# Repeating the products of twelve pairs of maximum blocks behind the last expert tile

## What is computed

```python
# convolution stage, per image
x = group_norm(hidden, pre) + pos_emb
gate = sigmoid(conv(silu(conv(silu(conv(x)))))); enhanced = x * gate
sh = group_norm(x, norm)                               # 1024 tokens x 128 channels
standard = attention(sh @ wq, sh @ wk, sh @ wv)        # 8 heads of 16
multi = two attentions of 64: queries from enhanced, keys and values from sh
x = group_norm(out_w(ff_w2(silu(ff_w1([standard, multi])))), post) + hidden
# token attention
t = x as tokens; t = t + attention(layer_norm(t), 8 heads of 16)
# experts
t = t + sum over the 2 chosen of 8 experts of w2(gelu(w1(layer_norm(t))))
```

## Time and profile before

| | |
|---|---|
| median of 3 runs | 3732.41 us |
| lowest and highest | 3728.28 and 3738.99 us |
| profiled execution | 3718.79 us |
| its span (first to last instruction) | 3717.0 us |
| mean granted TensorE clock over the span | 0.901 |
| busy: TensorE, VectorE, ScalarE, GpSimd | 82%, 61%, 47%, 17% |

### The profile page before, as it was taken

One profiled execution on the slowest core, in us unless ns is written; L12 is line 12 of the kernel. 1 busy time (PEld: TensorE's weight loads), 2 busy tenths in 40 slices (PEclk: granted clock), 3 DMA queues, 4 the chain that ended last, 5 costly groups with the idle time before them and its releaser, 6 DMA issues. The chain is left out here.

```text
span 3717.0 us, 43766 instructions
## 1 busy us (share of the span) xinstructions
PE 3063.4 (82%) x15438; PEld 1283.9 (35%) x15438; DVE 2274.4 (61%) x4359; ACT 1743.5 (47%) x2599; POOL 634.7 (17%) x558
## 2 busy tenths in 40 slices
PE   4789787988889898897879888897979978898855
PEld 1225322362223522253223622244322622235225
DVE  4753867457672777538674676737774486746750
ACT  1444354445554455443544455543644445444523
POOL 3010321004010220102210130102201032101322
PEclk9899799998998899997989989997999979898977
DMA  4014320063102620143300621025301532017125
GB/s 94 1 41 147 67 49 18 24 178 60 25 18 69 158 58 2 41 141 67 54 18 24 185 53 25 18 92 135 58 5 38 161 69 34 19 35 192 43 44 163
DMA packets 171289, 252.92 MB, mean 68 GB/s; under 512 B 25899, under 2 KB 79991, under 8 KB 170871
## 3 DMA queue, kind: packets, MB, share of 16 engines
q1 hardware_dynamic: 161791, 230.58, 25.0%
q0 software_dynamic: 9216, 18.89, 2.0%
HBM read 192.55 MB, written 56.83 MB: 67 GB/s over the span
## 5 line engine op out<-in xcount | busy, mean ns | idle before, releaser
L1268 DVE TENSOR_REDUCE blockmax<-ps 128x1 f32<-128x512 f32 x1912 | 1256.0, 685 | 565.4 <-PE ps L689 486.4
L1101 ACT ACTIVATE prob<-ps 128x1024 f32<-128x1024 f32 x1024 | 996.9, 1020 | 619.6 <-PE ps L861 522.2
L689 PE MATMUL ps<-ks,qs 96*128 96x512 bf16 x1656 | 677.6, 421 | 318.9 <-DVE blockmax L1268 205.9
L861 PE MATMUL ps<-qs,ks 99*128 99x512 bf16 x2048 | 653.4, 404 | 10.6 <-DMA qs<-maxrow_dram 7.6
L689 PEld LDWEIGHTS ps<-ks,qs 96*128 96x128 bf16 x1656 | 162.4, 102 | 1029.9 <-DVE blockmax L1268 777.7
L578 POOL TENSOR_TENSOR rs<-vn,vec 128x1 f32<-128x1 f32 (+1 forms) x43 | 42.8, 996 | 1707.9 <-DVE vn L1223 1196.9
L1145 ACT ACTIVATE prob<-ps,b1t 128x128 f32<-128x128 f32 x828 | 235.8, 368 | 164.2 <-PE ps L953 163.9
L861 PEld LDWEIGHTS ps<-qs,ks 99*128 99x128 bf16 x2048 | 206.2, 103 | 281.5 <-issue 88.7
L875 PE MATMUL ps<-prob,va_b 128*32 128x512 f32 x2048 | 291.9, 644 | 0.0
L875 PE MATMUL ps<-prob,va_a 128*32 128x512 f32 x2048 | 286.6, 633 | 0.0
L914 PE MATMUL ps<-qm,km 65*128 65x512 f32 x512 | 270.5, 654 | 3.6 <-ACT prob L1101 3.6
(11 more groups left out here) (227 smaller groups left out, 3315.5 us busy)
## 6 DMA issues: line engine op xcount, KB each, us to landing
shared<-in_w SPq DMA_DIRECT2D x108, 256.0 KB
prob<-in_w SPq DMA_DIRECT2D x108, 256.0 KB, 3.5
parts_dram<-parts SPq DMA_DIRECT2D x34, 768.0 KB, 4.4
ks<-parts_dram SPq DMA_DIRECT2D x204, 128.0 KB, 5.0
qs<-parts_dram SPq DMA_DIRECT2D x204, 128.0 KB, 7.4
qm<-in_w SPq DMA_DIRECT2D x90, 256.0 KB, 3.6
xe<-in_w SPq DMA_DIRECT2D x54, 256.0 KB
oatt<-in_w SPq DMA_DIRECT2D x54, 256.0 KB, 3.3
```

The costliest lines, as they stand in the source:

```text
L689: pe.matmul(ps[:, MX + n % 2, :], lhs, rhs, start=True, stop=True).then_inc(blocks_ready[f], 1)
L861: mm = pe.matmul(ps[:, SC + h, :], ks[:, slot_of(a, g), h, t * P:(t + 1) * P], qs[:, slot_of(a, g), h, cols(q)], start=True, stop=True)
L1101: act.activation(prob[:, n % 3, 2 * pr:2 * pr + 2, :], ps[:, SC + 2 * pr:SC + 2 * pr + 2, :], ACT.Exp, scale=HD ** -0.5).then_inc(exp_done ...
L1268: dve.tensor_reduce(blockmax[:, unit_of(j), cell_of(j), k:k + 1], ps[:, MX + n % 2, :], AX.X, ALU.max).then_inc(blocks_used[f], 1)
```

## The change

Pairs 0 to 15 stay as they are. For each of the pairs 16 to 27 the two products are issued three times, with the same operands and into the same banks. Every product starts its sum anew (`start=True`), so the last round leaves the same numbers. Only the two products of the last round signal `blocks_ready`.

```diff
+                def product(i):
+                    rows = slice(32 * (h + i), 32 * (h + i + 1))
+                    return pe.matmul(early_banks(d)[:, i, :], parts[rows, 1, 0, tile * P:(tile + 1) * P],
+                                     k_even[rows, cols(k)], start=True, stop=True)
+
+                if d >= UNDER_EXPERTS:
+
+                    for r in range(2):
+                        for i in range(2):
+                            product(i)
                 for i in range(2):
-                    rows = slice(32 * (h + i), 32 * (h + i + 1))
-                    pe.matmul(early_banks(d)[:, i, :], parts[rows, 1, 0, tile * P:(tile + 1) * P],
-                              k_even[rows, cols(k)], start=True, stop=True).then_inc(blocks_ready["b"], 1)
+                    product(i).then_inc(blocks_ready["b"], 1)
```

## The result

The median is **3786.25 us** (3778.89 to 3793.19, 4 runs) against 3730.35 us for the kernel before (3724.88 to 3738.99, 4 runs on the same chip). The ratio is 1.0147, 95% interval 1.0115 to 1.0180: slower, and 36 us above the forecast range. The profiled execution took 3778.89 us, with a span of 3777.1 us, 60.1 us more than before, and a mean granted clock of 0.896.

The account below looks back on a forecast made before the run. VectorE's reductions, 1.13 us apart, were taken to bound pairs 16 to 27 and hide the added products. Pair 16's 0.35 us in four images made 1.4 us, taken as 1: median plus 1, 3733 us, range 3718 to 3750.

Parts of the forecast that it names:

- 2.13 - 1.43 - 0.14 = 0.56 us: Pairs 19 on: TensorE's lead less a changed pair's duration and its signal; ready 0.56 us before VectorE wants it.
- The 0.14 us of a signal: From finished product to VectorE's reduction: estimated at 0.05 to 0.14 us from products at 378.77; 0.14 taken.
- the prediction had 0.35: Pair 16, not covered by reductions: ready 0.35 us late, so the last reduction ends 0.35 us later.
- the cover at 1.7 us: Images 1, 2, 6 and 7: GpSimd's own work hides the 0.35 us delay, with a lead of 1.7 us or more.
- the power's lead: Opening of the token attention: VectorE's variance was ready 1.76 us before GpSimd took it in image 1.
- the stall: TensorE's wait in step 2, 5.0 to 6.7 us; predicted to end 0.35 us later in images 3, 4, 5, 8.
- The rounds overlap: Pairs 16 to 27: rounds start 0.40 us apart at 1.2 GHz, so a changed pair lasts 1.43 us.
- The clock: Rival: busier TensorE brings the clock back for the token attention's opening; 3.2 us faster, to 3729; chance 0.09.
- The mix of long and short images: Width-64 attentions: images 1 and 2 went the long way at a lower clock, 7 us more per image.
- clock rival: Width-64 attentions: slow images turn fast (-14 us, 0.11), or more go the long way (+14 us from two, 0.16).
- Rounds that don't overlap: Rival: a pair's six products run one after another, 2.4 us a pair; 108 us slower, 3841; chance 0.02.
- distances other than 430 and 437 us: Sign of a wrong forecast: time from pair 27 to the next image's pair 27 leaving 430 and 437 us.

Follow-up runs that it names:

- the narrow rounds: The change with its two extra rounds 64 columns wide instead of 512, same number of instructions; 3800.60 us, 1.0160 against the kernel before.
- the single signal: The change, with only the last product of each pair signalling, by two at once; 3804.09 us, 1.0138 against the kernel before.
- ScalarE's copies: The kernel before, without extra products, plus 36 one-column copies on idle ScalarE once pair 20 is reduced; 3773.31 us, 1.0064.

## Why the prediction was wrong

**The step that failed.** "I take 0.14. So from pair 19 on each pair is ready 2.13 - 1.43 - 0.14 = 0.56 us before VectorE wants it: 48 products an image at nothing, hidden by the reductions." The 0.14 us of a signal came from a moment at which nothing else of this kind was going on the earlier trace rows. Beside the gather the signal of pair 26 in image 1 came 11.4 us behind its products. The cost is 10.3 us an image ahead of the reductions where the prediction had 0.35. That the gather is needed for it is shown (moved, the idle time falls from 89.9 to 8.9 us, and the same 48 products cost 2.2 us). That it does not go by columns or by signals is shown by the narrow rounds and the single signal; more instructions cost more (28, 69 and 84 us of idle time for 6, 12 and 24 extra products in pairs 22 to 27), but only late in the gather. SyncE's transfers are not needed for it. That it is not in TensorE alone is shown by ScalarE's copies, which are held up themselves and make a signal of TensorE's late behind the pairs. That the copies' slots and the pairs' late signals are one mechanism is argued: both come up only beside the gather.

**The size of what GpSimd hides.** I put the cover at 1.7 us in four images, from the power's lead, and wrote that the power would come as before, 17 us behind the last reduction. It waited for the variance instead (8.09 us in image 1), 13.9 us behind it. The earlier end of the stall gave back 23.5 us over eight images, 3 us in each, but against 82.8.

**What held.** L712 x832. The rounds overlap: 18 products in 2.74 us in image 2, at 1.2 GHz, where six rounds on one row group make 5 x 0.40 + 0.63 = 2.63. Pair 16 waits 0.30 us against the predicted 0.35, in six images; in images 1 and 4 the clock was still up when its products ran (18 products in 1.47 us) and it waits nothing. Image 2:

```profile
828.85 2.74 PE L712 MATMUL ps<-k_even,parts 32*128 32x512 bf16 x18 [1.21 <-DVE blockmax L1287]
...
830.44 2.36 DVE L1287 TENSOR_REDUCE blockmax<-ps 128x2 f32<-128x1024 f32 x2 [0.30 <-PE ps L712]
```

So the prediction's claim that the clock is at 0.50 there in all eight images holds for the kernel before alone. For pairs 16 to 21 by themselves "at nothing" was right: 1.0015, an interval that includes 1. With the gather out of the way the whole forecast fits: 2.2 us between two medians whose intervals overlap, where I had 1.

**The rivals.** The clock: 0.50 while the late pairs run, and 0.54 over the first 10.1 us of the opening where it had been 0.50, so it did not come back for the opening. The mix of long and short images stayed two to five, so neither clock rival came up. Rounds that don't overlap would have shown as long products; they are not. The text itself said that distances other than 430 and 437 us would mean a cost that I miss. That is what they were.

**Open.** What it is that each instruction sends out. Every run here was also recorded by the profiler, so it may be the records themselves, and no run here can tell whether an unrecorded execution would lose the 56 us. The missing events of signals speak for it, since they show the recording in trouble in just this stretch, but they don't show that it holds an engine up. The Trainium skill, page "NOTIFIC — the notification-queue block", section "7.1 Overflow: three behaviours, one of which stalls the engine", says that the internal pipeline of the block that writes such records pushes back on its producers rather than lose one. That would fit engines that stand still while every record of their instructions arrives; the events of signals were lost all the same, and no run here shows which block lost them. Open too is why it is the issuing rather than the landing of the indirect transfers that the late pairs follow (2.9 to 3.3 us behind its end), which was read from the traces and not tried apart. And why pair 24 is the first late one even where pairs 16 to 21 have no extra rounds, and why 96 instructions were free where 60 were not.

## To carry to other kernels

A latency read from a quiet moment, such as the 0.14 us of a signal here, did not hold beside a burst of GpSimd's indirect transfers; look at what every other engine does in the stretch before costing short instructions at nothing. Where an engine is idle, its operands are ready by the records, and the profile gives "remote" or "issue" as releaser, look for gaps in even steps and move the suspected burst away: that one experiment told more than five that varied the suspect. Count the trace's events too: where some are missing, the recording may be part of what is measured. None of these kernels beats the one before; moving the gather behind the pairs clears the signals but costs 2.8%.

## Unexpected behaviour of the hardware

- Beside 16 indirect transfers of GpSimd (one every 1.25 us), one-column copies of ScalarE that had started 0.1 us apart went to starts at multiples of 0.70 us after the first 22 to 26. VectorE stood still for 4.14 us in the same stretch, behind a product that had been done for 4.4 us. With the gather moved, all 36 took 3.47 us.
- TensorE's products went on at their pace in this state (30 in 5.99 us), while the signal of pair 26 in image 1 came 11.4 us late. VectorE's signal to TensorE took 0.06 us in the same stretch. Six extra products an image beside the gather cost 28 us of idle time in eight images, 12 (of one extra round, pairs 22 to 27) 69 us, and 24 some 84 us; with these the last late pairs came 3 us behind the end of GpSimd's issuing.
- The trace of the kernel before lacks 8 to 10 of TensorE's 24 signals an image for these pairs and 5 to 7 of VectorE's 12. With the gather moved it lacks none.
